# A decoder layer on one core: attention's turned exponentials computed as a second, transposed score product

## What is computed

```
kqv = x @ Wqkv + bqkv                      # heads of 32, 16 heads
scores = einsum('bsnh,btnh->bnst', k, q) / sqrt(32)
scores = triu(scores) - 10000 * tril(ones, k=-1)
attn   = softmax(scores, axis=2)           # over s, the first index
out    = einsum('bnkq,bknh->bqnh', attn, v) @ Wo + bo
x = layernorm(x + out)
x = layernorm(x + wkv(w, u, x, ctx))       # a recurrence along the tokens
x = layernorm(x + (silu(x @ Wg) * (x @ Wu)) @ Wd)
```

## Time and profile before

| | |
|---|---|
| median of 3 runs | 719.03 us (717.31 to 719.5) |
| the profiled execution: its own time | 717.3 us, the lowest of the runs shown |
| its span, first to last instruction | 717.3 us |
| instructions | 13042 |
| mean granted TensorE clock | 0.998 of full speed |

### The profile page before, as it was taken

How to read it: one execution, slowest core, us unless ns; L and a number is a source line. 1 busy time by engine, 2 the same in 40 slices (tenths; PEclk the granted TensorE clock), 3 DMA queues, 4 the chain that set the end, 5 groups by cost and what they waited for, 6 DMA issues and landing times. The chain is left out here.

```text
span 717.3 us, 13042 instructions
## 1 busy us (share of the span) xinstructions
PE 694.5 (97%) x4658; PEld 427.9 (60%) x4658; DVE 552.5 (77%) x1252; ACT 457.5 (64%) x1072; POOL 314.9 (44%) x352
## 2 busy tenths in 40 slices
PE   8899999999999999999999999999999799999997
PEld 3466665666666666656555454544455697578855
DVE  4567666879899988899945899998898786466644
ACT  5689885779887678768756744356552566346620
POOL 2015340455677342442345756576675243203321
PEclk9999999999999999999999999999999999999999
DMA  7846891343243043228026010000001000010001
GB/s 254 265 150 160 241 211 53 110 128 89 81 126 95 24 136 116 55 65 177 2 33 143 1 60 15 30 16 0 1 1 45 16 2 1 1 60 1 1 16 45
DMA packets 45538, 54.24 MB, mean 76 GB/s; under 512 B 4897, under 2 KB 34849, under 8 KB 45473
## 3 DMA queue, kind: packets, MB, share of 16 engines
q1 hardware_dynamic: 41632, 46.59, 21.2%
q0 software_dynamic: 3264, 6.29, 5.3%
q10 hardware_dynamic: 576, 0.52, 0.3%
HBM read 47.10 MB, written 12.58 MB: 83 GB/s over the span
## 5 line engine op out<-in xcount | busy, mean ns | idle before, releaser
L1422 DVE CUSTOM_DVE_ANT_0 ee<-psb,mask,clip 128x512 f32<-128x512 f32 (+3 forms) x256 | 131.1, 536 | 28.9 <-PE psb L974 28.3
L1201 ACT ACTIVATE ee<-ee,nm 128x512 f32<-128x512 f32 (+3 forms) x256 | 143.0, 561 | 1.4 <-DVE nm L1422 1.4
L1813 POOL TENSOR_TENSOR hl<-ring,hh 128x512 f16<-128x512 f32 x64 | 77.3, 1220 | 103.6 <-ACT hh L1315 61.3
L1212 ACT ACTIVATE ee<-psb 128x512 f32<-128x512 f32 (+1 forms) x172 | 87.1, 525 | 38.5 <-PE psb L985 33.4
L985 PE MATMUL psb<-ident,ee 128*128 128x128 f32 x640 | 97.6, 274 | 3.2 <-ACT ee L1212 3.0
L1110 PE MATMUL psb<-wd,hl 128*128 128x512 f16 x240 | 91.0, 379 | 0.6 <-POOL hl L1813 0.6
L1108 PE MATMUL psb<-wd,hh 128*128 128x512 f16 x240 | 91.0, 379 | 0.0
L985 PEld LDWEIGHTS psb<-ident,ee 128*128 128x128 f32 x640 | 75.6, 141 | 24.5 <-ACT ee L1212 6.0
L974 PE MATMUL psb<-ks,qs 128*128 128x512 f16 (+3 forms) x256 | 72.0, 301 | 2.7 <-DVE nm L1422 1.3
L1521 DVE RECIPROCAL ek<-ek 128x128 f32<-128x128 f32 x64 | 58.2, 931 | 6.5 <-POOL ek L1781 6.5
L932 PE MATMUL psb<-xh,wqk 128*128 128x512 f16 x240 | 59.8, 379 | 0.4 <-ACT wqk L1178 0.4
(11 more groups left out here) (205 smaller groups left out, 1614.4 us busy)
## 6 DMA issues: line engine op xcount, KB each, us to landing
qs<-parts SPq DMA_DIRECT2D x64, 128.0 KB, 2.8
ks<-parts SPq DMA_DIRECT2D x60, 128.0 KB, 3.0
parts<-qhl SPq DMA_DIRECT2D x16, 256.0 KB, 2.2
parts<-khl SPq DMA_DIRECT2D x16, 256.0 KB, 2.4
x<-in_x SPq DMA_DIRECT2D x4, 1024.0 KB, 8.3
ct<-in_ctxT SPq DMA_DIRECT2D x4, 1024.0 KB, 5.8
out<-x SPq DMA_DIRECT2D x16, 256.0 KB, 2.0
xt<-in_xT SPq DMA_DIRECT2D x14, 256.0 KB, 3.6
```

The source lines that it names most:

```text
L1201: e.activation(dst, dst, ACT.Exp, bias=NM[:, n % 4, col:col + 1], scale=-1.0, accum_out=DEN[:, n % 4, col:col + 1]).then_inc(sem("exp"), 1)
L1212: e.activation(ET[h][:, base:base + width], PSB[:, bank["turn", H, item], 0:width], ACT.Copy).then_inc(sem("et"), 1)
L1422: e.tensor_tensor_reduce(E[H % 3][:, EOFF[i]:EOFF[i] + w], PSB[:, bank["score", H, i], 0:w], MASK[:, S - w:S], -SC, CLIP[:, i:i + 1], ALU. ...
L1813: e.tensor_tensor(HS[it][1][:], pair(b, it // 2)[:, it % 2, :] if b in SEVEN else ring(b, it)[1], HS[it][0][:], ALU.subtract).then_inc(sem ...
```

## The change

1. `turn` (L1042 now) no longer transposes the exponentials. It computes the scores a second time with the operands exchanged, so that they come out transposed: four 16-bit products to a head, 512, 384, 256 and 128 columns, in the same three items and two banks.
2. The row maximum must be subtracted before the exponential, and in the transposed layout it differs along the columns. It is carried in the product: `stack(n)` fills only three combinations of halves (96 rows; the fourth, low times low, is dropped). The last 32 rows of k's operand hold the constant -4096, those of q's operand are zero for the first scores and are then overwritten by the maximum, scaled by 1/(SC x 16 x 4096), as 16 equal rows of its high half and 16 of its low half.
3. To get there: `mq` (DVE, two operations 128x16), `mt` (PE, one product against a 16-bit identity, 32x128), `mrow` (ACT, 32x128), `mput` on SP: a write to a scratch in DRAM (`shifts`), a wait for it, and two broadcast reads of 16 rows each. The first transposed score of a group waits for these reads.
4. `et` (ACT, L1273) is now the exponential instead of a copy, and all 192 items are on ACT. `exp` stays as it was, for the row sums; what it writes is read by nobody.
5. The triangle of the diagonal blocks is cut by `mask` on POOL (L1832, `affine_select`), two to a head, 256 elements each; `pv` waits for them.
6. Buffers: `E` has two slots (so `weigh` of head H waits for `exp` of head H - 2), `ET` five, q and k operands three.
7. The timetable is new throughout. Eight feed-forward pieces of batch 0 instead of four lie between slots 246 and 276, `TURN_AT`, `PV_AT`, `SV_AT` and others are given for each group, four halves `oh` and four `xh` go from ACT to POOL.

The diff, cut to its core (in the tables, a line or two of each):

```diff
+M_ROWS, M_SCALE = 16, 4096.0
+M_UNIT = 1.0 / (SC * M_ROWS * M_SCALE)
+E_SLOTS, ET_SLOTS, QK_SLOTS = 2, 5, 3
...
-EARLY = 4
+EARLY = 8
...
-TURN = ((7, 6, 5), (4, 5, 7), (4, 5, 6), (2, 4, 4))
-COPIES = (0, 0, 0, 0, 6, 0, 0, 0, 0, 0, 0, 0, 4, 0, 0, 3)
+TURN_AT = {0: ((20, 21, 25), (22, 25, 26), (27, 29, 32), (31, 31, 32)), 1: ((21, 22, 22), (25, 25, 31), (23, 29,
...
+MQ_AT = {0: 12, 1: 28, 2: 44, 3: 60, 4: 76, 5: 92, 6: 108, 7: 124, 8: 140, 9: 156, 10: 172, 11: 188, 12: 204, 13:
...
+MT_AT = {0: 13, 1: 29, 2: 46, 3: 60, 4: 77, 5: 93, 6: 109, 7: 125, 8: 143, 9: 157, 10: 173, 11: 189, 12: 205, 13:
...
+    def turned(H, item):
+        add("et", H, item)
+        for half in (0, 1):
+            if item in (half, half + 1) and {("et", H, half), ("et", H, half + 1)} <= tt.place.keys():
+                add("mask", H, half)
+
+    def shifts(n):
+        tt.unit("mt", n)
+        add("mt", n)
+        add("mrow", n)
+        add("mput", n)
...
         def score(H, i):
             n, h = divmod(H, 4)
-            sl, w = n % 2, P * (i + 1)
+            w = P * (i + 1)
             emptied(("score", H, i))
             pe.wait_ge(*by_stack(n, "q"))
             pe.wait_ge(*by_stack(n, "k"))
-            e.matmul(PSB[:, bank["score", H, i], 0:w], QS[:, sl, h, i * P:(i + 1) * P], KS[:, sl, h, 0:w],
-                     start=True, stop=True).then_inc(sem("score"), 1)
+            pe.wait_ge(*by_made("rows"))
+            e.matmul(PSB[:, bank["score", H, i], 0:w], heads(n, "q")[:, h, i * P:(i + 1) * P],
+                     heads(n, "k")[:, h, 0:w], start=True, stop=True).then_inc(sem("score"), 1)
+
+        def shift_rows(n):
+            emptied(("mt", n))
+            pe.wait_ge(*by_shift(n))
+            pe.wait_ge(*by_made("ident16"))
+            e.matmul(PSB[0:32, bank["mt", n], 0:P], MHL[:, n % 2, :], IDENT16[:], start=True,
+                     stop=True).then_inc(sem("mt"), 1)
 
         def turn(H, item):
+            n, h = divmod(H, 4)
             bk, base = bank["turn", H, item], TBASE[item]
-            blocks = [(j, i) for j in TRI[item] for i in range(j, T)]
             emptied(("turn", H, item))
-            pe.wait_ge(*by("exp", H, min(i for _, i in blocks)))
-            pe.wait_ge(*by_consts())
-            for j, i in blocks:
-                o = TOFF[j] - base + (i - j) * P
-                mm = e.transpose(PSB[:, bk, o:o + P], E[H % 3][:, EOFF[i] + j * P:EOFF[i] + (j + 1) * P], IDENT[:])
+            pe.wait_ge(*by_mstack(n))
+            for j in TRI[item]:
+                o = TOFF[j] - base
+                mm = e.matmul(PSB[:, bk, o:o + (T - j) * P], heads(n, "k")[:, h, j * P:(j + 1) * P],
+                              heads(n, "q")[:, h, j * P:S], start=True, stop=True)
             mm.then_inc(sem("turn"), 1)
...
         def et(H, item):
-            n, h = divmod(H, 4)
             base, width = TBASE[item], P * sum(T - j for j in TRI[item])
             act.wait_ge(*by("turn", H, item))
-            if n:
-                act.wait_ge(*by("pv", n - 1))
+            if H >= ET_SLOTS:
+                act.wait_ge(*by("pv", (H - ET_SLOTS) // 4))
             else:
                 act.wait_ge(*by("split_w", 4))
-            e.activation(ET[h][:, base:base + width], PSB[:, bank["turn", H, item], 0:width],
-                         ACT.Copy).then_inc(sem("et"), 1)
+            e.activation(ET[H % ET_SLOTS][:, base:base + width], PSB[:, bank["turn", H, item], 0:width], ACT.Exp,
+                         scale=SC).then_inc(sem("et"), 1)
+
+        def shift_rows(n):
+            act.wait_ge(*by("mt", n))
+            if n:
+                act.wait_ge(*by_mput(n - 1))
+            e.activation(MROW[:], PSB[0:32, bank["mt", n], 0:P], ACT.Copy).then_inc(sem("mrow"), 1)
...
-            if H >= 3:
-                for item in range(3):
-                    dve.wait_ge(*by("turn", H - 3, item))
+            if H >= E_SLOTS:
+                dve.wait_ge(*by("exp", H - E_SLOTS, 0))
...
+        def shift(n):
+            high, low = MHL[:, n % 2, 0:16], MHL[:, n % 2, 16:32]
+            dve.wait_ge(*by("weigh", 4 * n + 3, 0))
+            if n >= 2:
+                dve.wait_ge(*by("mt", n - 2))
+            e.tensor_scalar(high, NM[:, n % 4, :], -M_UNIT, None, ALU.mult).then_inc(sem("mq"), 1)
+            dve.wait_ge(*by_shift(n, False))
+            e.scalar_tensor_tensor(out=low, in0=NM[:, n % 4, :], scalar=-M_UNIT, in1=high, op0=ALU.mult,
+                                   op1=ALU.subtract).then_inc(sem("mq"), 1)
...
+        def mask(H, half):
+            a0, step = ((TOFF[3], P), (0, S))[half]
+            pool.wait_ge(*by("et", H, half))
+            pool.wait_ge(*by("et", H, half + 1))
+            block = ET[H % ET_SLOTS][:, a0:a0 + 2 * step].rearrange("p (j t) -> p j t", j=2)[:, :, 0:P]
+            e.affine_select(block, block, [[0, 2], [1, P]], ALU.is_ge, 0.0, base=0,
+                            channel_multiplier=-1).then_inc(sem("mask"), 1)
...
         def stack(n):
+            if n >= QK_SLOTS:
+                sp.wait_ge(*by_turned(n - QK_SLOTS))
+            sp.wait_ge(*by_consts())
             if n >= 2:
-                sp.wait_ge(*by("score", 4 * (n - 2) + 3, 0))
+                sp.wait_ge(*by_mstack(n - 2))
             for kind in ("q", "k") if n else ("q",):
                 sp.wait_ge(*by_put(n, kind))
-                for r in range(4):
+                if kind == "q":
+                    e.dma_start(heads(n, "q")[3 * 32:P, :, :],
+                                MASK[3 * 32:P, 0:S // 2].bitcast(F16).unsqueeze(1).broadcast_to([32, 4, S])).then_inc(sem(f"stackq{n % 2}"), 16)
+                for r in range(3):
                     e.dma_start(*stacked(n, kind, r)).then_inc(sem(f"stack{kind}{n % 2}"), 16)
+
+        def put_shifts(n):
+            sp.wait_ge(*by("mrow", n))
+            e.dma_start(MSCR[n].rearrange("k h (i t) -> (k h i) t", i=T), MROW[:]).then_inc(sem("mput"), 16)
+            sp.wait_ge(*by_mput(n))
+            for k in (0, 1):
+                a0 = 3 * 32 + M_ROWS * k
+                e.dma_start(heads(n, "q")[a0:a0 + M_ROWS, :, :],
+                            MSCR[n, k].unsqueeze(0).broadcast_to([M_ROWS, 4, S])).then_inc(sem(f"stackq{n % 2}"), 16)
```

More of the change, by code:

```diff
@@ L82 @@
+WU_AT = (41, 48, 48, 51)
 WU_ZERO = (56, 124, 127, 150)
[L83 to L92 removed]
@@ L494, in spread_over @@
         for k, u in enumerate(units):
-            at(first + k * (end - first) // len(units), u)
+            at(first + k * max(end - first, 0) // len(units), u)
     def piece(slot, *what):
@@ L521, in timetable @@
     spread_over([u for it in range(EARLY) for u in gu_parts(0, it, (GBANK, GBANK))], *EARLY_AT)
+    for k in range(T):
+        piece(WD_AT[k], "load_f", "wd", k)
     for what in ("load_second", "small", "load_ds"):
@@ L546, in timetable, with value_sums, values, close @@
     for H in range(NHG):
+        n, h = divmod(H, 4)
         for item in range(3):
[L548 to L567 removed]
+            turns.setdefault(16 * n + TURN_AT[n][h][item], []).append((H, item))
+    def value_sums(n):
+        tt.unit("sv", n)
+        add("sv", n)
+        late(WAIT["t1"], lambda: add("t1", n))
+    def values(n):
+        tt.unit("pv", n)
+        add("pv", n)
+        late(WAIT["t1"], lambda: add("t2", n))
+    def close(n):
+        spread(n, 1)
+        late(WAIT["t3"], lambda: add("t3", n))
+        late(WAIT["oh"], lambda: add("oh", n))
+        late(WAIT["ol"], lambda: add("ol", n))
+    fin = {}
+    for n in range(NG):
+        for slot, what in ((EX_AT[n], lambda n=n: add("expand", n)), (SV_AT[n], lambda n=n: value_sums(n)),
+                           (SPREAD_AT[n], lambda n=n: spread(n, 0)), (PV_AT[n], lambda n=n: values(n)),
+                           (WIDE_AT[n], lambda n=n: close(n))):
+            fin.setdefault(slot, []).append(what)
+    shift = {}
+    for n in range(NG):
+        shift.setdefault(MQ_AT[n], []).append(lambda n=n: add("mq", n))
+        shift.setdefault(MT_AT[n], []).append(lambda n=n: shifts(n))
+    wo3 = wo_units(B - 1)
+    for t in range(T):
+        for u in wo3[3 * t:3 * t + 3]:
+            at(FF + WO_IN[t], u)
+    for it in range(IT):
+        at(FF + ZERO_IN[it], lambda it=it: add("zero", "wd", it))
+    at(PV_AT[NG - 1], lambda: add("load_ct", 2))
+    for n in range(NG + 2):
         for slot in range(16):
+            if 16 * n + slot >= 16 * NG + TAIL:
+                break
             h, k = divmod(slot, 4)
@@ L777, in by_stack, with by_made, by_shift, by_turned @@
     def by_stack(n, kind):
-        return sem(f"stack{kind}{n % 2}"), 64 * (n // 2 + 1)
+        return sem(f"stack{kind}{n % 2}"), 64 + 96 * (n // 2) if kind == "q" else 48 + 48 * (n // 2)
+    def by_made(what):
+        return sem("made"), {"nt": 1, "zp": 2, "rows": 4, "ident16": 5, "half": 6, "edge": 8}[what]
+    def by_shift(n, low=True):
+        return sem("mq"), 2 * n + 1 + low
+    def by_turned(n):
```

(18 more changed lines are left out.)

249 lines of the change are left out of this document (118 added, 131 removed), and 9 rows, old and new, of the table TURN_AT.

## The result

The changed kernel takes 735.81 us (median of 4 runs, 734.92 to 737.21); the kernel before, run beside it, 718.33 (717.31 to 719.5). The ratio is 1.024, 95% interval 1.0219 to 1.0262: **slower**, where 701 us was forecast. The profiled execution has a span of 733.9 us.

The account below looks back on a forecast made before the run. PE, busy 97%, was taken as the bound, with ACT and then DVE taking over in the attention. 21.6 + 294 + 383.6 = 699.2 us, with 1.7 for the median 701; range 684 to 717 (the forecast's own 693 to 711).

Parts of the forecast that it names:

- Turns to transposed scores, -34.1 us on PE: PE in the attention: 69.8 us of turns go, 34.8 of transposed scores and 0.9 of `mt` come.
- `et` +0.092 us each: ACT: exponential instead of copy costs 0.092 us more for each of 192 items, 1.1 us a group.
- the 143 of the forecast: First half of the attention, 21.6 to 183.2 us: ACT's busy time, against PE's 141, so ACT takes over.
- Masks 0.41 us: POOL: 128 mask operations at 0.41 us (bounds 0.22 to 1.22), 3.3 us a group, taken as hidden.
- The maxima at nothing: Attention: chain from `mt` to landed reads, 5.6 us, covered by 6.5 us of other PE work, so costed at nothing.
- Stacks are issued over ten slots ahead of use, which covers it: SP: two more DMAs and a 2.2 us pause per group, said to be covered by the stacks' early issue.
- 97% for two engines near the limit, attention 294 us: Attention: ACT, then DVE sets the pace, at 97%: 147 + 147 = 294 us, 23.6 less.
- The rest, 383.6 us: After group 15's first score: 378.1 less 2.1 for turns plus 7.6 of PE work moved out of the attention.
- nothing added: The rest of the run: four more early pieces are work moved forward within it, at no cost.
- The signs: If right: ACT busy over 90% to group 8, DVE over 95% from there, group 15 at 315 to 317 us.
- the slower rival: Attention: maxima late in every group, holding PE before the first transposed score; 736 us, chance 12%.
- its turning point of 1.1 us a group: Late maxima make the kernel slower from 1.1 us a group above the forecast (18 / 16).

Follow-up runs that it names:

- e3: Changed kernel with each diagonal mask on POOL cut from 256 elements to 2: 730.46 us, ratio 1.0169.
- e2: Changed kernel with the maxima's whole way left out (split, `mt`, `mrow`, write and reads): 724.9 us, ratio 1.0088.
- e9: Changed kernel with three of four `wu` loads moved behind group 4's first scores and its stack at slot 48 instead of 51: 726.07 us, ratio 1.0101.
- e5: Kernel before the change, its own order, with only 5 of 10 turns per head from head 4 on: 707.98 us, ratio 0.9858.
- e16: e5 with ACT's `ET` copies over 128 columns from head 4 on and DVE's reciprocals over 16 columns: 692.26 us, ratio 0.9627.
- e7: Changed kernel with the recurrence's reciprocals on DVE over 16 of 128 columns: 723.83 us, ratio 1.0068.
- e8: Changed kernel with ACT's `ET` exponentials over 128 columns from head 5 on and DVE's reciprocals over 16 columns: 720.96 us, ratio 1.0031.
- e15: e9 with four early gate and up pieces ahead of the tail instead of eight: 743.76 us, ratio 1.032.
- e10: Changed kernel with `mt` of every group one slot later on PE: 743.73 us, ratio 1.036.
- e11: Changed kernel with the edits of e2, e3 and e9 in one: 717.29 us, ratio 0.9982.
- e13: e9 with transposed scores of groups 0, 8, 12, 13 spread over the slots and group 10's stack at slot 145 instead of 148: 727.61 us, ratio 1.0117.

## Why the prediction was wrong, step by step

- **Turns to transposed scores, -34.1 us on PE: right.** The usual distances fell by 33.2. 128 columns are followed after 0.056 us here too, as against the 81 ns of the Trainium skill (TensorE: Matmul & The Clock Gate, Back-to-back issue gap); the trace does not agree with that figure.
- **`et` +0.092 us each: wrong, nearly harmless.** It costs nothing (592 against 599 ns), the low end of its bounds; the row that was taken, L1240, has a bias operand, and L1186 with one takes 684 ns without being an exponential. ACT's work did not grow: 251.5 us in the attention against 254.0, and 126.4 up to group 8 against the 143 of the forecast. With PE's 141 in its place the forecast would have been some 2 us lower still.
- **Masks 0.41 us: right in size (0.439), wrong as "hidden".** They cost 5.4 us (e3), at least in part through `pv`. The sentence that `pv` waits for the last one was in the forecast, and no price was put on it.
- **The maxima at nothing: wrong.** The chain (5.6 forecast, 5.7 measured) and its cover (6.5 forecast, 8.2 measured, with PE's own waits in it) were about right, and group 13, named for its cover of 3.8 us, is the one where PE waits for a read. Not seen was that PE waits at `mt` itself for the split on DVE behind the group's last `weigh`, that SP waits in order for `mrow`, and that the work is in ACT's and DVE's queues too: 10.9 us in all (e2). How this sum splits was not tried.
- **"Stacks are issued over ten slots ahead of use, which covers it": the step that failed at one place, at 9.7 us (e9).** Counted in the kernel's own timetable it is 9 slots for group 4, and over ten for only three of groups 2 to 15. The landing was that of the earlier trace rows and worse, 11 us instead of 5 to 8.5, for three loads of `wu` were issued within 2.1 us of each other, just ahead of the stack. The price was in the rows; it was applied to the maxima and not to the stack.
- **97% for two engines near the limit, attention 294 us: the step that failed most.** e5, with nothing new but less PE work, has 306.7 where the rule gives 293, (141.6 of PE in the first half + 142.6 of DVE in the second) / 0.97. Busy of DVE over the stretch, or of ACT, is no bound from which 3% gives the time: three engines in order that wait for each other by turns lose time although none is full. The waits of PE grew by 18 us as soon as its work fell by 33, and lighter ACT and DVE bring back only 9.4 us of the attention (e16).
- **The rest, 383.6 us: measured 393.8.** In the trace 3.0 of these 10.2 us are the new wait for the recurrence at 494 us, and some 4.5 are half clock, there and at 578 us. e2 takes 4.7 away. Lighter DVE and ACT take 12.7 and 13.4 (e7, e8), but with the 5 us for snapshots that the kernel before loses too. e15 shows also that "nothing added" undervalued the early pieces.
- **The signs.** No engine is where they wanted it: ACT 76 and 84% up to group 8 (forecast over 90), DVE 93 and 89% after it (over 95), group 15 at 340.1 us (315 to 317). PE waits 1.2 us for a read of `shifts`, so the sign of the slower rival is absent but for this. That the result, 735.8, is the rival's 736 is chance. e10, one slot later, brings on what the rival described, in five groups and for 7.9 us; its turning point of 1.1 us a group was not tested.

Account in us: 32.7 less PE work in the old order gives 719.1 to 708.0 (e5). The new order without the maxima, the masks' work and the collision at the stack gives 717.3 (e11); in the profiled executions 8 of the difference are half clock. These three bring it to 735.8. How far the 9 us between e5 and e11 belong to the ring of buffers, the tail or the first groups stays open.

## What to carry to other kernels

When the bounding engine gets lighter, each wait that its work had covered comes into view, and the gain is not "until the next engine is full": remove the work without its replacement, as in e5, and see how much is there at all (here a third). Price every new dependency at the place where an in-order engine stands before it, not only over its own chain, and give each buffer ring's earliest start the landing times of the busiest stretch. A wait of PE can be paid twice, once itself and once in the half clock behind it; which waits are, their sum does not tell (42.2 us of waits with 5.6 of half clock in e5, 45.5 with 13.6 in e11). And before a price is taken from a row, look at all its operands: a bias can cost what is put down to the function.

## What was not expected of the hardware

- An ACT exponential from PSUM to SBUF takes the time of a copy of the same shape (592 and 599 ns for 512 columns, 381 and 386 for 256). What has a bias operand takes longer, whatever its function: 691 ns for the exponentials L1240, 684 for L1186, which only adds the bias.
- Copies of 128 KB landed in 5.4 us behind one load of 1 MB (e9), and in 11 us where three loads of 512 KB, issued within 2.1 us of each other, stood ahead of them as well.
- Seven times the granted clock fell to half, 1.2 GHz, at a loss of 1.0 to 3.0 us each; the kernel before has one such stretch. Spreading the transposed scores (e13) took 5.4 us of half clock away and added 5.1 of waits.
